# A later fetch of a root weight, and a new order of split, scale and merge steps, in a fused graph network kernel

## What is computed

```
w    = einsum('rb,bio->rio', att, basis)          # 30 bases of 512 x 512, twice
gate = sigmoid(x_j @ gate_w[r, :, 0])
msg  = gate[:, None] * x_j @ w[r]                 # for each of two relations
h    = relu(segment_sum(msg, row) + x @ root + bias)
out  = the same with the second set of weights, on h
x    = layernorm(x + out)
```

## Time and profile before

| | |
|---|---|
| median of 3 runs | 296.14 us (295.69 to 296.43) |
| the profiled execution's own time | 296.78 us |
| its span, first to last instruction | 295.0 us |
| TensorE busy | 268.2 us, 91% |
| VectorE busy | 169.4 us, 57% |
| ScalarE busy | 82.5 us, 28% |
| GpSimd busy | 49.9 us, 17% |
| DMA | 74.15 MB, 251 GB/s on the mean |

### The profile page before, as it was taken

The page is one execution under the profiler, slowest core; times in us unless marked ns, Lnnn a source line. Parts: engine busy times, 40 slices in busy tenths (PEclk is TensorE's granted clock), DMA queues, the critical chain, the costliest instruction groups (busy, mean ns, idle before and its releaser), DMA issues.

```text
span 295.0 us, 4587 instructions
## 1 busy us (share of the span) xinstructions
PE 268.2 (91%) x1661; PEld 179.1 (61%) x1661; DVE 169.4 (57%) x361; ACT 82.5 (28%) x140; POOL 49.9 (17%) x92
## 2 busy tenths in 40 slices
PE   0899898999999897998999998999999999999991
PEld 0793433434567562664455574677997778777770
DVE  6788878887758769948885314112333243234443
ACT  2442021002546864186441400120032332000000
POOL 5531000000395002012510000000009100011111
PEclk9999999999799999999999999999999999999998
DMA  6999999999799999999899999990004200001112
GB/s 161 212 402 400 420 364 385 408 403 360 281 322 291 357 421 398 397 343 417 341 367 411 377 365 331 400 344 18 2 1 113 67 0 0 0 2 35 35 35 69
DMA packets 12963, 74.15 MB, mean 251 GB/s; under 512 B 2034, under 2 KB 2277, under 8 KB 4748
## 3 DMA queue, kind: packets, MB, share of 16 engines
q1 hardware_dynamic: 11330, 70.82, 63.8%
q0 software_dynamic: 1264, 2.87, 3.9%
q10 hardware_dynamic: 346, 0.17, 0.2%
HBM read 72.57 MB, written 1.28 MB: 250 GB/s over the span
## 4 chain that ended last, share of the span: by engine, by line
PE 63%; DMA 16%; DVE 10%; issue 4%; ACT 2%; POOL 1%; DVEq 1%; SPq 0%; POOLq 0%; ACTq 0%
DMA basis_ring<-in_L_gnn_basis_dram 14%; PE psW L560 12%; PE psM L541 9%; PE psM L542 8%; PE psM L543 8%; PE psM L819 7%; PE psM L845 6%; PE psE L647 3%; DMA xs<-in_x_dram 3%; PE psM L690 2%; DVE B L1170 2%; PE psM L600 2%; PE psM L614 1%; DVE zg L1347 1%; DVE hlT L1321 1%
## 5 line engine op out<-in xcount | busy, mean ns | idle before, releaser
L560 PE MATMUL psW<-basis_ring,S 128*32 128x512 f32 x512 | 64.2, 613 | 4.5 <-DMA basis_ring<-in_L_gnn_basis_dram 4.0
L560 PEld LDWEIGHTS psW<-basis_ring,S 128*32 128x32 f32 x512 | 13.1, 110 | 33.2 <-issue 20.8
L1347 DVE SCALAR_TENSOR_TENSOR zg<-psM,gate,zg 125x512 fp32r<-125x512 f32 x20 | 15.0, 750 | 31.2 <-ACT zg L1006 31.0
L647 PEld LDWEIGHTS psE<-oh_key,oh_src 128*125 128x125 f16 x162 | 14.5, 147 | 18.3 <-issue 13.7
L819 PE MATMUL psM<-BB,zg 125*128 125x320 f32 (+1 forms) x160 | 24.3, 306 | 0.0
L845 PE MATMUL psM<-zg,BB 125*125 125x512 f32 x100 | 24.0, 394 | 0.0
L1006 ACT ACTIVATE zg<-psM,gate 125x512 fp32r<-125x512 f32 x20 | 13.6, 687 | 35.9 <-PE psM L543 35.5
L819 PEld LDWEIGHTS psM<-BB,zg 125*128 125x128 f32 x160 | 23.4, 189 | 0.0
L1404 DVE TENSOR_SCALAR h_full<-psM,vecT 128x320 f32<-128x320 f32 (+1 forms) x8 | 4.3, 542 | 32.5 <-PE psM L819 28.7
L1170 DVE TENSOR_TENSOR B<-B,psE 125x160 f32 x54 | 17.4, 323 | 8.5 <-issue 3.7
L845 PEld LDWEIGHTS psM<-zg,BB 125*125 125x125 f32 x100 | 18.6, 186 | 4.7
(11 more groups left out here) (164 smaller groups left out, 454.5 us busy)
## 6 DMA issues: line engine op xcount, KB each, us to landing
basis_ring<-in_L_gnn_basis_dram SPq DMA_DIRECT2D x64, 1024.0 KB, 8.0
root_raw<-in_L_gnn_root_dram POOLq DMA_DIRECT2D x32, 64.0 KB, 4.2
xs<-in_x_dram SPq DMA_DIRECT2D x1, 1120.0 KB
out_dram<-xs SPq DMA_DIRECT2D x5, 224.0 KB
w_raw<-in_L_gnn_W_dram SPq DMA_DIRECT2D x4, 256.0 KB, 9.6
gate_raw<-in_L_gnn_gate_w_dram POOLq DMA_DIRECT2D x2, 250.0 KB, 8.3
bias_b<-in_L_gnn_bias_dram POOLq DMA_DIRECT2D x1, 250.0 KB, 3.8
xs<-in_x_dram SPq DMA_DIRECT2D x1, 130.0 KB
```

Of the source, the lines that this page charges most:

```text
L560: m = nc.tensor.matmul(psW[32 * j:32 * j + 32, cc % 2, :], S[:, cc % 2, cc // CH, q].rearrange("p k r -> p (k r)"), ring[:, n % RING, j, : ...
L647: nc.tensor.matmul(psE[0:PC, g % 2, at:at + KEYS], oh_src[:, g % 3, j * P:j * P + PC], oh_key[:, t % OH, :], start=(j % SG == 0), stop=(j ...
L1347: link(v.scalar_tensor_tensor(out=zg[:, 1, c, r, :], in0=bank(("Z", L, c, r))[0:PC, :], scalar=gate[:, L, c, r:r + 1], in1=zg[:, 0, c, r, ...
```

## The change

Four things are changed, and no arithmetic.

1. GpSimd issues the 16 transfers of the root weight behind the layer norm's power for chunk 2, instead of ahead of the batch norm's powers. `root1_low(0)` moves behind all five powers.
2. The parts of the basis behind the eight h steps go from (53, 57, 59, 61, 63) to (53, 55, 57, 59, 61, 63): two behind each of the first six steps.
3. ScalarE gets one more sigmoid, on two constant columns, ahead of the first `x1_out`. In the loop over chunks, both `z_scaled` of a chunk come ahead of `x1_hi(c + 2)` and `x1_out(c + 3)`, and `root1_high` and `w_high(4)` move to later chunks.
4. VectorE does both `z_part` of a chunk together, then the next chunk's gates, then `w_merge` or `w_low`, then `x1_lo(c + 2)` and `spread_of(c + 3)`. The split of the gate weights `gw_hl` moves ahead of the loop.

```diff
-            for kc in range(KC):
-                for j in range(JB):
-                    pool.dma_start(root1_raw[32 * j:32 * j + 32, kc],
-                                   root1.rearrange("(k c j) o -> c j k o", k=2 * KB, c=KC)[kc, j]) \
-                        .then_inc(root1_in, 16)
             for f in range(KC):
                 pool.wait_ge(var_ready, f + 1)
                 inverse_root(bn[:, 2, f:f + 1], 1)
...
                 if c == 2:
-                    root1_low(0)
-            for k in range(1, KC):
+                    for kc in range(KC):
+                        for j in range(JB):
+                            pool.dma_start(root1_raw[32 * j:32 * j + 32, kc],
+                                           root1.rearrange("(k c j) o -> c j k o", k=2 * KB, c=KC)[kc, j]) \
+                                .then_inc(root1_in, 16)
+            for k in range(KC):
                 root1_low(k)
...
-                    basis_upto((53, 57, 59, 61, 63, 63, 63, 63)[KC * h + f])
+                    basis_upto((53, 55, 57, 59, 61, 63, 63, 63)[KC * h + f])
...
+            nc.scalar.activation(gate[:, 1, 0], mhalf[0:PC, 0:R], ACT.Sigmoid)
             x1_out(0)
...
+            x1_hi(1)
+            x1_out(2)
             for c in range(NC):
-                if c == 0:
-                    x1_hi(1)
-                if 0 < c + 2 < NC and c < 1:
-                    x1_out(c + 2)
                 act.wait_ge(gate_dots, R * (c + 1))
                 link(nc.scalar.activation(gate[:, 0, c], gate[:, 0, c], ACT.Sigmoid))
                 act.sem_inc(gate_ready, 1)
                 z_scaled(0, c, 0)
-                if 1 <= c < NC - 1:
-                    x1_hi(c + 1)
-                    if c + 2 < NC:
-                        x1_out(c + 2)
+                if c == 2:
+                    root1_high(0)
+                elif c == 3:
+                    root1_high(2)
+                elif c == 4:
+                    w_high(4)
                 z_scaled(0, c, 1)
                 if c == 0:
                     w_first(4)
-                    root1_high(0)
-                elif c == 1:
+                elif c == 2:
                     root1_high(1)
-                    root1_high(2)
-                elif c == 2:
+                    w_first(5)
+                elif c == 3:
                     root1_high(3)
-                    w_high(4)
-                    w_first(5)
                 elif c == 4:
                     w_high(5)
                     w_first(6)
+                if c + 2 < NC:
+                    x1_hi(c + 2)
+                if c + 3 < NC:
+                    x1_out(c + 3)
...
                 dve.wait_ge(gate_ready, c + 1)
                 dve.wait_ge(x1_ready, min(c + 2, NC))
-                z_part(0, c, 0)
-                if 1 <= c < NC - 1:
-                    x1_lo(c + 1)
+                for r in range(R):
+                    z_part(0, c, r)
                 if c + 1 < NC:
                     gates_dotted(c + 1)
+                if c == 1:
+                    w_merge(4)
+                elif c == 3:
+                    w_merge(5)
+                elif c == 4:
+                    w_low(4)
+                    w_low(5)
+                if c + 2 < NC:
+                    x1_lo(c + 2)
                 if c + 3 < NC:
                     spread_of(c + 3)
-                z_part(0, c, 1)
```

More of the change, by code:

```diff
@@ L1368, in _ @@
             gates_dotted(0)
+            gw = vecT[:, :, V_GATE:V_GATE + 2 * R].rearrange("p k (l r) -> p l k r", l=2)
+            link(v.tensor_copy(gw_hl[:, :, :, 0], gw))
+            v.tensor_tensor(gw_hl[:, :, :, 1], gw, gw_hl[:, :, :, 0].bitcast(F32), ALU.subtract).then_inc(gw_ready, 1)
             for c in range(NC):
@@ L1384, in _ @@
                     link(last)
[L1385 to L1395, removed]
             for h, (a, n) in enumerate(HALF):
```

## The result

The changed kernel took 298.4 us (median of 22 runs, 296.56 to 300.35), the kernel before 296.71 (22 runs). The ratio is 1.0052, 95% interval 1.003 to 1.0074: slower by half a per cent, where the prediction had it 0.3% faster, and outside its range by 0.4 us. The profiled execution of the changed kernel took 299.83 us with a span of 298.0, 3.0 more than before.

The account below looks back on a forecast made before the run. TensorE and the DMA engines were both near their limit ahead of 168 us, TensorE alone from 206. Gains 1.2 + 2.1 + 1.7 = 5.0 us against a 4.9 us fetch price left 0.8 net: 295.3 us, range 291.8 to 298.0.

Parts of the forecast that it names:

- TensorE loses 0.9 us up to there: Up to part 51: with a fetch price of 4.9 us it lands at 167.8 us, against 166.9 before.
- 3 to 5: Between 133 and 165 us: TensorE should wait for the basis several times, 3 to 5 us in all.
- the gain of 1.2 us ahead of Z: Start of the products Z: 1.2 us sooner, since the basis load for 101.44 us is no longer late.
- my rivals: Fetch mostly hidden, chance 0.27; fetch costs more than its own time, 0.20; GpSimd's queue decides, 0.08.
- the prediction's list of what to look for: Signs in the changed profile: places of basis and low-half waits, the table load, load 51's landing, h step times.
- The fetch's old place: Near 101 us: without the fetch the basis wait of 1.45 us goes; gain 1.2 us.
- The order of ScalarE and VectorE: Chunk loop: low-half waits of 1.44 and 0.64 us go, table load hidden ahead of `x1_out(0)`; gain 2.1 us.
- GpSimd's queue: Layer norm: issues of 7.84 us covered, costing nothing; as rival, late root weight or issues give 297.3 us, chance 0.08.
- The h steps: Basis parts behind the h steps: waits of 1.28 and 0.40 us go; gain 1.7 us.
- The price of the fetch: Basis stream from load 38 to part 51: the fetch delays it by 4.9 us, between 4.0 and 5.6.
- the forecast's own sum: At part 51: wanted at 163.6 us, landing at 162.9 without the fetch; late by the fetch's price less 0.7 us.
- the forecast 167.8: Landing of part 51 with the fetch at a price of 4.9 us: 162.9 + 4.9 = 167.8 us.

Follow-up runs that it names:

- Two pairs of runs: Changed kernel without and with twelve unread matmuls ahead of part 41: 298.4, 296.86 us; fetch behind load 33 plus a held TensorE wait, empty and filled: 297.89, 296.1 us.
- the version with the h steps alone: The kernel before with only the new places of the basis parts behind the h steps: 295.43 us, ratio 0.9993.
- few bytes: The changed kernel with the same 16 transfers, each with 16 of the 512 columns, GpSimd clearing the rest of the tile: 292.2 us, ratio 0.9857 to the kernel before.
- the filled wait: The changed kernel with twelve matmuls that nobody reads ahead of part 41, where TensorE waited for the basis: 296.86 us, ratio 1.0022 to the kernel before.
- the fetch behind load 33: The changed kernel with the fetch issued in SyncE's own queue behind basis load 33, GpSimd having no part in it: 292.9 us, ratio 0.9896 to the kernel before.
- behind load 37: The changed kernel with the fetch issued in SyncE's own queue behind basis load 37: 294.92 us, ratio 0.995 to the kernel before.
- the empty held wait: The version with the fetch behind load 33, plus a TensorE wait ahead of part 41 for small GpSimd operations: 297.89 us, ratio 1.0053 to the kernel before.

## Why the prediction was wrong

**The step that failed** is "TensorE loses 0.9 us up to there": I counted TensorE's waits for the fetch at their own length and nothing for what follows them. The waits were there as forecast, 4.1 us where I had said 3 to 5. But 3.2 of them came at one place, and with it the granted clock went to its lower level for 6.7 us in both profiles of the changed kernel, some 2.9 us of lost work. The profiled pair can be added up at the first matmuls with scaled messages, in the first h step:

```profile
169.73 3.11 PE L819 MATMUL psM<-BB,zg 125*128 125x320 f32 x20
...
174.64 3.11 PE L818 MATMUL psM<-BB,zg 125*128 125x320 f32 x20
```

They start 4.9 us later than before (first line), where 0.9 was forecast. The waits for the basis brought 4.1 us, as in the forecast, and the waits for the low half that went took off 2.1. The clock added 2.9 us, which I had at nothing, and the gain of 1.2 us ahead of Z is missing. Behind this point the 1.7 us of waits at the h steps went, and in the end the span is 3.0 us longer.

Two pairs of runs bear the clock out: filled, the wait leaves it whole (the change of the time lies inside the noise there), and a wait with no transfer in it brings the fall, which filling takes away again, this time with times that lie apart. None of my rivals had it, and the prediction's list of what to look for did not name the clock. The clock is not all: with the wait filled the kernel takes 296.86, 0.2% over the kernel before, where the forecast was 0.3% under it. Some of this half a per cent is the price of the fetch, below; the rest, why the clock does not fall in all executions, and how long it stays down, stay open.

In the changed kernel's trace TensorE waited 3.16 us for a load at 144.49, the granted clock fell within that wait, and eight matmuls behind it took 1.93 us instead of 1.07. The Trainium skill (TensorE: Matmul & The Clock Gate, "HAM oscillation — how this bites in real kernels") describes such a case: an engine that waits for the next operand's transfer long enough has its clock lowered, and the work behind the wait starts slow. The trace agrees, with these numbers; the prediction should have weighed it and did not.

**The fetch's old place.** The wait at 101.44 went, as forecast. But Z starts at 117.64 in the changed kernel's profile, against 117.61 before, so the gain of 1.2 us does not show there. The reason lies ahead of the fetch's old place, where TensorE is early or late by up to 1.8 us from one execution to another (the lower clock at 76 to 88 us lasted 3.4 us in the profile before and 6.7 in that of the changed kernel). The same matmuls in the kernel before, in the changed kernel and in the version with the h steps alone:

```profile
88.74 0.44 PE L704 MATMUL psM<-ident,B 125*125 125x125 bf16 x4 [0.41 <-DVEq L1282]
...
89.86 0.45 PE L703 MATMUL psM<-ident,B 125*125 125x125 bf16 x4 [0.41 <-DVEq L1283]
...
90.02 0.44 PE L704 MATMUL psM<-ident,B 125*125 125x125 bf16 x4 [0.41 <-DVEq L1282]
```

From them to the start of Z it is 28.9 us before and 27.8 in the changed kernel, and 27.7 with few bytes and with the filled wait, where Z starts at 115.96 and 116.23. So the term is 1.1 us, as good as forecast. It is won only where TensorE would have come early, though: in the version with the h steps alone, which has the fetch in its old place, TensorE was 1.3 us later here, and it had no wait near 101 at all (also 27.7 us). I had read the wait of one execution as that of all.

**The order of ScalarE and VectorE.** Right. No wait for the low half is left behind the first chunk. The table load lies in the idle time ahead of `x1_out(0)`, at 111.16, 2.07 us of which are left:

```profile
111.16 1.28 ACT L980 ACT_TABLE_LOAD   x1
...
114.73 0.81 ACT L969 ACTIVATE xs<-x_sum,lnm,lrs 125x512 f32<-125x512 f32 x1 [2.07 <-POOL lnm L511]
...
135.25 0.81 ACT L969 ACTIVATE xs<-x_sum,lnm,lrs 125x512 f32<-125x512 f32 x1 [4.85 <-POOL lnm L511]
```

`x1_out(3)` came at 135.25, not 133.9, since the fetch's issues began at 126.4; TensorE still did not wait for it. GpSimd's queue decided nothing.

**The h steps.** The waits went. Their 1.7 us are in the profile, but not shown as a time by themselves.

**The price of the fetch.** It was set too low, and the changed kernel's 4.1 us of waits hide this, by luck: TensorE came to them more than a us later than forecast. In the version with the filled wait it came on time, waited 1.8 us and was filled for 3.1, 4.9 us in all where 4.2 was forecast. By the forecast's own sum that is a price of 5.6, not 4.9. The runs do not settle how it comes about. The issue and landing of loads 38 and 51, with few bytes, with the full fetch and the filled wait, and with the fetch behind load 33, where it has landed before:

```profile
L417 SPq DMA_DIRECT2D basis_ring<-in_L_gnn_basis_dram x1: 328/328/328, 123.3 to 123.3; - x1
...
DMA to landing us min/median/max: 4.8/4.8/4.8
...
L417 SPq DMA_DIRECT2D basis_ring<-in_L_gnn_basis_dram x1: 328/328/328, 154.9 to 154.9; - x1
...
DMA to landing us min/median/max: 9.4/9.4/9.4
```

```profile
L417 SPq DMA_DIRECT2D basis_ring<-in_L_gnn_basis_dram x1: 328/328/328, 123.6 to 123.6; - x1
...
DMA to landing us min/median/max: 4.7/4.7/4.7
...
L417 SPq DMA_DIRECT2D basis_ring<-in_L_gnn_basis_dram x1: 328/328/328, 159.9 to 159.9; - x1
...
DMA to landing us min/median/max: 8.5/8.5/8.5
```

```profile
L417 SPq DMA_DIRECT2D basis_ring<-in_L_gnn_basis_dram x1: 328/328/328, 123.4 to 123.4; - x1
...
DMA to landing us min/median/max: 6.5/6.5/6.5
...
L417 SPq DMA_DIRECT2D basis_ring<-in_L_gnn_basis_dram x1: 328/328/328, 154.9 to 154.9; - x1
...
DMA to landing us min/median/max: 8.6/8.6/8.6
```

With the fetch between them the 13 loads take 40.1 us. Without it they take 36.2 in one profile and 33.6 in the other, where I had 34.2. So the net price up to part 51 is 3.9 us by the first and 6.5 by the second, on both sides of my 4.9. Part 51 landed at 168.4 us with the filled wait, against the forecast 167.8; in the changed kernel, where the slow TensorE also frees the ring's places later, at 171.4.

What I missed is how the price is spread. In the changed kernel load 38 landed at 129.8 (125.0 and 4.8) and load 41 at 144.4 (131.1 and 13.3), 14.6 us for three loads that take 7.5 at 2.5 us each: 7.1 us late at once (with few bytes the three took 9.1 us). That concentration made the one long wait. In SyncE's queue the same bytes cost 3.7 us, so about half of the 7.1 seems to be the running side by side.

## What to carry to other kernels

Where a bulk stream is at its limit, a side transfer belongs where TensorE has loads in store, and in the stream's own queue: the same 1.05 MB was 0.5% slower than before in one place and, in the stream's queue and issued 20 us sooner, 1.0% faster. When a wait of TensorE is priced, read the clock behind it as well as the wait: here one wait of 3 us cost 5 to 6, while single ones of 1 to 1.5 us left the clock whole. A wait in one profile can be taken up by how early TensorE came to it, so look at a second execution before counting it as a gain. And the slack of the loads is not a sum to draw on: the fetch split over the batch norm used up 2 to 6 us of it and made waits of 4.6.

## What the runs showed of the hardware

- The granted clock was at its lower level for 3.4 to 6.7 us behind single waits of TensorE of 2.4 to 3.2 us, whatever was waited for (a load or GpSimd), or from the last us of such a wait on, and at its full level behind single waits of 0.6 to 1.8 us. It also fell for 3.4 us behind two waits of 0.9 us that lie 1.6 us apart, ahead of 108.4 and 110.0 us with the fetch behind the power of chunk 1, ahead of 108.9 and 110.6 with it behind load 37, and ahead of 109.3 and 110.9 with the empty held wait; in the changed kernel and in the versions with few bytes, with the filled wait and with the fetch behind load 33 the same pair left the clock whole. Twelve matmuls in a wait kept it up. A long wait is not needed for a fall: every profile has one of 3.4 or 6.7 us between 76 and 88 us (in the kernel before a mean of 0.86 over these 12 us, in the changed one 0.72), and in the kernel before TensorE had waited no longer than 0.4 us at a time in the 8 us ahead of it.
- Transfers issued by GpSimd beside SyncE's loads went with a rate of 304 GB/s, against 412 behind them, at a DMA share of 1.0; they made the stream late by 7.1 us for 1.05 MB in the changed kernel. In SyncE's queue the rate fell too, to 273 GB/s for some 4 us, and the same transfers cost 3.7 us.
- 16 transfers of 64 KB took SyncE 8.2 us to issue ahead of load 24, no less than the 7.84 us of GpSimd.
